# Order of the head columns in the features pass, and which engines write the three parts of the features

## The reference

```python
def _feature_map(x, gamma, beta):
    mu = x.mean(axis=-1, keepdims=True)
    var = ((x - mu) ** 2).mean(axis=-1, keepdims=True)
    xn = (x - mu) / jnp.sqrt(var + LN_EPS) * gamma + beta
    ...
q = (hidden_states @ Wq.T).reshape(b, t, HEADS, FEAT).transpose(0, 2, 1, 3)
k = (hidden_states @ Wk.T).reshape(b, t, HEADS, FEAT).transpose(0, 2, 1, 3)
```

## Time and profile before

| | |
|---|---|
| median of 3 runs | 3000.76 us |
| lowest and highest | 2988.22 and 3003.45 us |
| the profiled execution | 2993.09 us |
| its span, first to last instruction | 2991.4 us |
| mean granted TensorE clock | 0.936 |
| busy in the span | PE 84%, DVE 76%, ACT 60%, POOL 18% |
| features pass, its projections and after | about 1797 to 2098 us |

### The profile page before, as it was taken

The page is one execution under the profiler, slowest core; times in us unless marked ns, Lnnn a source line. Parts: engine busy times, 40 slices in busy tenths (PEclk is TensorE's granted clock), DMA queues, the critical chain, the costliest instruction groups (busy, mean ns, idle before and its releaser), DMA issues. The chain is left out here.

```text
span 2991.4 us, 60704 instructions
## 1 busy us (share of the span) xinstructions
PE 2506.4 (84%) x15239; PEld 1153.1 (39%) x15239; DVE 2285.2 (76%) x5907; ACT 1785.1 (60%) x2938; POOL 542.1 (18%) x636
## 2 busy tenths in 40 slices
PE   2783999999999999577999988775699999995656
PEld 1441233333333333164666665453122222222545
DVE  5896888888888888276777767998666666665968
ACT  0451466666666666415777746664577777773446
POOL 0341111211112111140000001223122222222300
PEclk9896799999999999788999998998799999998879
DMA  5486223233232332150000002444544444442403
GB/s 167 160 268 191 68 72 106 82 95 93 84 106 83 95 94 83 57 179 22 0 0 0 0 0 78 158 157 159 152 138 139 139 138 140 138 136 92 144 18 112
DMA packets 246389, 309.99 MB, mean 104 GB/s; under 512 B 42544, under 2 KB 180480, under 8 KB 246272
## 3 DMA queue, kind: packets, MB, share of 16 engines
q1 hardware_dynamic: 246272, 308.82, 33.5%
HBM read 181.29 MB, written 126.88 MB: 103 GB/s over the span
## 5 line engine op out<-in xcount | busy, mean ns | idle before, releaser
L840 ACT ACTIVATE a_p<-psum 128x1024 f32<-128x1024 f32 (+3 forms) x768 | 588.7, 813 | 303.9 <-PE psum L945 299.0
L840 ACT ACTIVATE b_p<-psum 128x512 f32<-128x512 f32 (+5 forms) x768 | 453.5, 654 | 169.1 <-PE psum L945 168.2
L934 PE MATMUL psum<-a_ks,a_qs 112*128 112x512 bf16 (+3 forms) x1536 | 453.6, 340 | 100.9 <-DVE a_ks L862 43.6
L895 DVE CUSTOM_DVE_ANT_0 a_dump<-psum,a_bias 128x128 bf16<-128x128 f32 (+3 forms) x1024 | 444.7, 487 | 105.4 <-PE psum L934 72.9
L945 PE MATMUL psum<-a_qs,a_ks 114*128 114x512 bf16 (+3 forms) x1536 | 382.1, 331 | 5.6 <-ACT a_p L840 3.0
L945 PE MATMUL psum<-b_qs,b_ks 96*128 96x512 bf16 (+7 forms) x1536 | 320.9, 330 | 40.7 <-DMA b_vs<-values 40.4
L893 DVE TENSOR_REDUCE a_peak<-psum 128x1 f32<-128x512 f32 x512 | 327.0, 685 | 22.0 <-PE psum L934 20.1
L959 PE MATMUL psum<-b_p,b_vs 128*32 128x512 f32 (+3 forms) x3072 | 328.4, 500 | 8.0 <-POOL b_p L819 8.0
L959 PE MATMUL psum<-a_p,a_vs 128*32 128x512 f32 (+3 forms) x3072 | 332.4, 505 | 0.4 <-POOL a_p L819 0.4
L872 DVE COPY b_twin<-psum 128x512 f32<-128x512 f32 (+3 forms) x384 | 213.5, 556 | 147.4 <-PE psum L945 145.7
L819 POOL TENSOR_SCALAR_AFFINE_SELECT a_p<-a_p 128x512 f32<-128x512 f32 x256 | 162.4, 635 | 816.5 <-ACT a_p L840 816.5
(11 more groups left out here) (194 smaller groups left out, 3271.1 us busy)
## 6 DMA issues: line engine op xcount, KB each, us to landing
qk_parts<-l_parts SPq DMA_DIRECT2D x192, 128.0 KB
qk_parts<-g_parts SPq DMA_DIRECT2D x192, 128.0 KB, 1.7
a_qs<-qk_parts SPq DMA_DIRECT2D x160, 128.0 KB, 2.9
a_ks<-qk_parts SPq DMA_DIRECT2D x160, 128.0 KB, 3.0
b_qs<-qk_parts SPq DMA_DIRECT2D x160, 128.0 KB, 2.9
b_ks<-qk_parts SPq DMA_DIRECT2D x160, 128.0 KB, 3.0
values<-l_vx SPq DMA_DIRECT2D x64, 256.0 KB
a_vs<-values SPq DMA_DIRECT2D x32, 512.0 KB, 3.7
```

The lines of the kernel that those rows point to most:

```text
L840: act.activation(p[s % SLOTS][:, 2 * k:2 * k + heads, q0(s):512], m.psum[:, at:at + heads, q0(s):512], ACT.Exp if softmax else ACT.Square, ...
L895: last = dve.tensor_tensor_reduce(dump[c % SRING][:, at:at + w], piece, bias[:, 512 - w:], 1.0, NEG, ALU.add, ALU.max, dst)
L934: last = pe.matmul(m.bank[SB + c % SRING][:, at:at + w], qs[r][0:TOP, hd, qt * P:(qt + 1) * P], ks[r][0:TOP, hd, h * 512:h * 512 + w], sta ...
```

## The change

The weight columns of Q and K are put into position-major order while the weights are prepared (`heads_turned`), so the projection yields the columns in the order in which `g_qk` holds them; ACT's copy becomes plain, and the sums of squares and the subtraction of the means read with a step. ACT writes the high part straight from PSUM, by a second activation of each bank. DVE writes the low part. GpSimd has no program in this pass.

```diff
-            for w in range(4):
+            def heads_turned(w):
+                for c in range(z.DC):
+                    last = dve.tensor_copy(
+                        m.w_qkv[:, c, w * z.D:(w + 1) * z.D].rearrange("p (n d h) -> p n h d", d=z.DK, h=z.HPU),
+                        m.bank[w][:, c * z.D:(c + 1) * z.D].rearrange("p (n h d) -> p n h d", d=z.DK, h=z.HPU))
+                return last
+
+            for w in range(2):
+                take("qkv", lambda: heads_turned(w))
+            for w in range(2, 4):
...
-                view = m.w_qkv[:, c, 0:2 * z.D].rearrange("p (h f) -> p h f", f=z.DK)
-                mean = means[:, c * 2 * z.H:(c + 1) * 2 * z.H]
+                view = m.w_qkv[:, c, 0:2 * z.D].rearrange("p (n d h) -> p n h d", d=z.DK, h=z.HPU)
+                mean = means[:, c * 2 * z.H:(c + 1) * 2 * z.H].rearrange("p (n h) -> p n h", h=z.HPU)
                 did(dve.tensor_reduce(mean, view, AX.X, ALU.add))
                 did(dve.tensor_scalar(mean, mean, 1.0 / z.DK, None, ALU.mult))
-                did(dve.tensor_tensor(view, view, mean.unsqueeze(2).to_broadcast([P, 2 * z.H, z.DK]), ALU.subtract))
+                did(dve.tensor_tensor(view, view, mean.unsqueeze(3).to_broadcast([P, 2 * z.H // z.HPU, z.HPU, z.DK]),
+                                      ALU.subtract))
...
-                    dve.tensor_reduce(var[u][:, t, :], sq[t % 2][:, :].rearrange("p (h f) -> p h f", f=z.DK), AX.X,
-                                      ALU.add).then_inc(var_ready, 1)
+                    squares = sq[t % 2][:, :].rearrange("p (n d h) -> p n h d", d=z.DK, h=z.HPU)
+                    dve.tensor_reduce(var[u][:, t, :].rearrange("p (n h) -> p n h", h=z.HPU), squares, AX.X, ALU.add
+                                      ).then_inc(var_ready, 1)
...
                 dve.wait_ge(feat_ready, 4 * n + 6)
-                dve.wait_ge(stored[u], STORED * i + STORED)
-                dve.tensor_copy(parts[u][:, 0, :, :], feat[u][:, :, :]).then_inc(high_done, 1)
-                dve.wait_ge(high_done, n + 1)
                 dve.wait_ge(low_done, n + 1)
                 dve.tensor_tensor(rest[:, :, :], feat[u][:, :, :], parts[u][:, 0, :, :], ALU.subtract).then_inc(rest_done, 1)
                 dve.wait_ge(rest_done, n + 3)
+                dve.wait_ge(stored[u], STORED * i + STORED)
                 dve.tensor_copy(parts[u][:, 1, :, :], rest[:, :, :]).then_inc(mid_done, 1)
+                dve.wait_ge(mid_done, n + 1)
+                dve.tensor_tensor(parts[u][:, 2, :, :], rest[:, :, :], parts[u][:, 1, :, :], ALU.subtract
+                                  ).then_inc(low_done, 1)
...
-        @block.gpsimd
-        def _(pool):
-            pool.sem_inc(low_done, 1)
-            with pool.Fori(0, GROUPS // 2) as i:
-                for u in range(2):
-                    n = 2 * i + u
-                    wait_alone(pool, mid_done, n + 1, m.alone)
-                    pool.tensor_tensor(parts[u][:, 2, :, :], rest[:, :, :], parts[u][:, 1, :, :], ALU.subtract
-                                       ).then_inc(low_done, 1)
...
-                    act.activation(qk[u][:, t, :].rearrange("p (n d h) -> p n h d", d=z.DK, h=z.HPU),
-                                   m.bank[Q0 + t % 2].rearrange("p (n h d) -> p n h d", d=z.DK, h=z.HPU), ACT.Copy
-                                   ).then_inc(qk_taken, 1)
+                    act.activation(qk[u][:, t, :], m.bank[Q0 + t % 2], ACT.Copy).then_inc(qk_taken, 1)
...
                 act.wait_ge(rest_done, n + 1)
+                act.wait_ge(stored[u], STORED * i + STORED)
                 for j in range(4):
                     act.wait_ge(ft_ready, 4 * n + j + 9)
-                    act.activation(feat[u][:, j, :], m.bank[F0 + j % 2], ACT.Identity, bias=m.beta_col[:, 0:1],
-                                   scale=m.gamma_col[:, 0:1]).then_inc(feat_ready, 1)
+                    for dst in (feat[u][:, j, :], parts[u][:, 0, j, :]):
+                        last = act.activation(dst, m.bank[F0 + j % 2], ACT.Identity, bias=m.beta_col[:, 0:1],
+                                              scale=m.gamma_col[:, 0:1])
+                    last.then_inc(feat_ready, 1)
```

More of the change, by code:

```diff
@@ L1441, in features_pass @@
         (raw_done, mv_ready, sd_ready, rs_ready, xn_ready, turned, xt_ready, qk_ready, qk_taken, sq_ready, var_ready,
-         hsd_ready, hrs_ready, qn_ready, ft_ready, feat_ready, high_done, rest_done, mid_done, low_done, v_ready,
+         hsd_ready, hrs_ready, qn_ready, ft_ready, feat_ready, rest_done, mid_done, low_done, v_ready,
          vx_ready, ones_ready) = sems(nc, *["g_" + x for x in (
              "raw_done", "mv_ready", "sd_ready", "rs_ready", "xn_ready", "turned", "xt_ready", "qk_ready", "qk_taken",
-             "sq_ready", "var_ready", "hsd_ready", "hrs_ready", "qn_ready", "ft_ready", "feat_ready", "high_done",
+             "sq_ready", "var_ready", "hsd_ready", "hrs_ready", "qn_ready", "ft_ready", "feat_ready",
              "rest_done", "mid_done", "low_done", "v_ready", "vx_ready", "ones_ready")])
@@ L1478, in _ @@
             dve.sem_inc(rest_done, 2)
+            dve.sem_inc(low_done, 1)
             def measure(i, u):
```

## The result

The changed kernel takes 3007.74 us (median of 20 runs, 2992.28 to 3019.87), the one before 2994.69 on the same chip (20 runs, 2988.1 to 3009.48). The ratio is 1.0046, 95% interval 1.0034 to 1.0058: 13 us slower, where 7.6 faster was forecast (2993.2, with a range of 2980 to 3006). The profiled execution took 3012.91 us, against 2993.09.

A forecast was written before the change was run, and what follows sets the result against it. DVE was taken to bound the features pass, before and after. Start +1.7, eleven steps -7.7, tail -3.9 and weights pass +2.3 gave -7.6 us, from 3000.8 to 2993.2 us, range 2980 to 3006.

The forecast's parts named there:

- DVE's sum: Features pass step on DVE: 17.04 - 3.22 - 1.25 + 2.33 = 14.90 us, with four dearer reductions 16.34.
- The block by GpSimd: Features pass: DVE's multiplies are blocked while GpSimd subtracts, 3.22 us of each step, gone with the change.
- The reduction's price: Features pass: each sum of squares reading at a 16-byte step costs 0.36 us more, four a step 1.44.
- ACT's 0.49 for its writes: Upper bound for a reduction's extra cost: what ACT pays writing 512 columns at that step, 1.099 against 0.607 us.
- four rivals: Other prices of the reductions or no bound by PE: 2983, 3000, 3013 and 2975 us; chances 0.18, 0.18, 0.10, 0.04.
- rivals 1 and 2: Reductions at full rate, -17.7 us, chance 0.18; reductions 0.49 us dearer as on ACT, -0.9 us, chance 0.18.
- PE's loop: Features pass: PE refills feature banks after ACT's reads; two extra reads make its step 15.69 us, hidden beside DVE's 16.34.
- Nothing outside it and the weights pass is touched: Whole kernel: the change affects only the features pass and the weights pass.
- The covers: Features pass: store buffers free at 13.7 us, before ACT wants them at 17.7, a cover of 4.0.
- the tail: Features pass after the twelfth split, steps chained by PE and ACT: 54.9 against 58.8 us, -3.9.
- the start: Features pass: the first split comes later by two extra reads and one dear reduction, +1.7 us.
- the eleven steps: Features pass, first to twelfth split: each step 16.34 instead of 17.04 us, -7.7 in all.

The follow-up runs named there:

- e1: Kernel before with only the column order changed, high cast still on DVE and low part on GpSimd: 3015.72 us, ratio 1.0087.
- e8: Kernel before with only the engines changed, ACT writing the high part once per group from SBUF after the four features: 2960.77 us, ratio 0.9902.
- e3: Changed kernel with a third PSUM bank for the features: 2989.84 us, ratio 1.0008 to the kernel before.
- e2: Kernel before with only the engines changed (second activation of each bank, low part on DVE, no GpSimd), old column order: 2996.03 us, ratio 1.0022.
- e12: Changed kernel run once more without edits: 3007.89 us, ratio 1.0048 to the kernel before.
- e5: Kernel before run once more without edits, on another chip: 2988.73 us, ratio 0.9999.
- e9: Changed kernel with two set-up memsets moved from DVE to GpSimd: 2995.32 us, ratio 1.0013 to the kernel before.

## Why the prediction was wrong

**DVE's sum held.** The block by GpSimd is real and goes with it: e1 keeps it (5.70 us for four), the changed kernel doesn't (2.50). The rule that the forecast cited from the Trainium skill, "SBUF — State Buffer", section "Who interferes with whom", agrees. High cast -1.25, low part +2.33 against 2.29 measured: right. The sum without the reductions was 14.90, and e8 ran at 14.93. The reduction's price was forecast at 0.36; it is 0.39 in the step by e1 (0.41 by its duration). ACT's 0.49 for its writes was no guide, L347 on the same engine was nearer. With that, DVE's step would be 14.90 + 1.56 = 16.46, and e3 shows 16.53. None of the four rivals came true as written: the price of 0.39 lies between rivals 1 and 2, and PE's loop was met.

**The step that failed** is "PE's own step becomes 14.37 + 2 x 0.66 = 15.69 us. It lies beside DVE's 16.34, hidden by it with 0.65 to spare." The two reads do stand ahead of the fourth fill, and PE does wait for the banks nearly twice as long (1.97 + 0.68, in most steps 1.72 + 0.68, against 1.39). But the sum took the loop's other terms at full clock. The reads split PE's time into wait, four transposes, wait, four transposes; behind that the clock falls to 0.50 in nine steps of eleven, and the first projection block then takes up to 1.56 us more. At full clock the loop is the forecast's, 15.78 in e2; with the falls in nine steps of eleven the mean is 17.07, above the 16.5 that DVE asks for. DVE's gain of 0.7 us a step was then no gain: the features pass was to become 9.9 us shorter, and it became 0.8 longer, or 2.1 shorter in e12 (302.6). e2, e3 and e8 show it from three sides: the step keeps its length with cheaper DVE work, and loses it as soon as the double reads no longer stand between the fills.

A sign of this was at hand. The features pass of before has a mean clock of 0.92 while the earlier trace rows show 1.00 for its middle. In the old trace the same first projection block takes 5.51 us at the pass's start (1806.42), behind waits of 13.41 and 2.99 us, and 5.30 near its end, behind one of 1.75:

```profile
2047.87 1.33 PE L1620 MATMUL psum<-ident,g_qk 128*128 128x128 f32 x8 [1.75 <-ACT g_feat L1579]
2049.03 5.30 PE L1603 MATMUL psum<-w_qkv,g_xt 128*128 128x512 f32 x8
```

The forecast named the clock of the middle and didn't ask what PE's new waits would do to it.

**"Nothing outside it and the weights pass is touched"** failed as well. The weights pass, forecast at +2.3, took +3.2 (78.6 against 75.4; 78.1 against 75.6 in e12 and e5): each halved copy 0.61, each strided reduction and subtraction 1.05. That is only a size. But its two additional copies stand ahead of the attention pass, and e9 and e12 measure 12.6 us for that (9.3 by the means). Together: 9 to 13 from these two instructions, some 8 to 11 missed in the features pass and 0.9 in the weights pass make 18 to 24, against a miss of 13.0 + 7.6 = 20.6. That the ratio, 0.46% above 1, lies within the 0.5% to which the forecast gave 0.68 is luck: its terms are not the ones that made it.

**The covers.** Store buffers came free in time: ACT waited for a DMA once, 7.2 us near the end, as the tail forecast. The other terms, by the same marks in the two traces: the start cost 0.7 us (forecast 1.7), the eleven steps 0.4 (forecast -7.7), the tail gave 0.3 (forecast 3.9). Start and tail were worked out with PE at full clock as well; no run takes them apart.

**What stays open.** e2's median lies 7.6 us above the old kernel's (the expectation said within 5), and its profile, of an execution of 2985.71 us, one of its fastest, shows no pass in which they went. e1 has the two instructions ahead as well, yet an attention pass of 991 us, with 27.3 us lost in all of which its features pass (+17.1) and weights pass (+3.3) explain 20. Why the clock falls in nine steps of the features pass and not in the other two, and why a second stop of half a microsecond costs nothing and one of 0.9 goes with twice the falls, isn't known. Not run: the full change with the high part copied late.

## What to carry to other kernels

Before an engine is given a second read of a PSUM bank that TensorE refills, write down TensorE's whole loop with its waits, and cost the work behind them at half clock too: here two waits, 2.40 to 2.65 us together, and the clock behind them took the gain of a correct DVE sum. A copy for another consumer is better taken from SBUF behind the last fill, even where it costs 1.91 us of an engine with time to spare. The fastest kernels here also keep the old order of the columns: the new one cost DVE 0.39 us in each of four reductions a step and saved ScalarE time that gained nothing: PE's loop at full clock takes 15.78 us in e2, 15.89 and 16.16 in the changed kernel. And a difference in a pass that the diff doesn't touch can be real: count the instructions that were added ahead of its loops, and move a few away before believing in noise.

## What was not expected of the hardware

- TensorE's waits of 1.72 to 1.97 and 0.68 us with four transposes between were followed by a fall of the clock from 1.00 to 0.50 in nine steps of eleven, which cost up to 1.56 us in the next block; the same waits left it at 1.00 in the other two. Behind one wait of 2.34 (e3) it fell in three steps of eleven, behind the 2.04 and 1.39 of before, with sixteen transposes between, in none.
- VectorE's sum over 16 positions, 512 f32 columns read at a step of 16 bytes, takes 1.088 us instead of 0.675. The Trainium skill, "Vector Engine (DVE) Microarchitecture Reference", section "Measured stream behaviour on trn2", gives 1.73 ns a column for an operation of two sources, one of which hops by 4 KiB at every element. Taken over for this step of 16 bytes, in place of the 1.05 it gives otherwise, that makes an estimated +0.35, where the runs show +0.39 to +0.41.
- Behind the jump back of a long loop VectorE stood still for 2.5 us in every kernel, and again for 0.18 to 1.05 us (median of a trace), the longer the more instructions (70 to 76 in the weights pass) stood ahead of the loop.
